# A message-passing layer with a running maximum: four exact lanes of 100,000 edges, a short last pair, one transfer for each load, x loaded earlier at the end, and the norm's small operands in PSUM

## The reference

```python
h = jnp.maximum(_layernorm(x, axis=-1), 0.0)
e_feat = jnp.concatenate([h[src], h[dst], edge_attr], axis=-1)   # 96 features
hid = jax.nn.relu(e_feat @ W1 + b1)                               # 64
v = hid @ W2 + b2                                                 # 32
x_cand = jax.ops.segment_max(v, dst, num_segments=12500)
out = x + jnp.maximum(x_cand, h)
```

## Time and profile before

| what | value |
|---|---|
| median of 3 runs | 3252.11 us (3249.76 to 3254.17) |
| the profiled execution: its own time | 3252.11 us |
| the profiled execution: span from first to last instruction | 3250.3 us |
| PE busy | 3011.4 us, 93% of the span |
| POOL busy | 2432.8 us, 75% |
| DVE busy, ACT busy | 2193.5 us and 2108.6 us, 67% and 65% |
| mean granted TensorE clock | 0.967 of full speed |

### The profile page before, as it was taken

How to read it: one execution, slowest core, us unless ns; L and a number is a source line. 1 busy time by engine, 2 the same in 40 slices (tenths; PEclk the granted TensorE clock), 3 DMA queues, 4 the chain that set the end, 5 groups by cost and what they waited for, 6 DMA issues and landing times.

```text
span 3250.3 us, 56988 instructions
## 1 busy us (share of the span) xinstructions
PE 3011.4 (93%) x19600; PEld 2222.8 (68%) x19600; DVE 2193.5 (67%) x2408; ACT 2108.6 (65%) x2462; POOL 2432.8 (75%) x2558
## 2 busy tenths in 40 slices
PE   6999999999999999999999999999998998999800
PEld 4777677777777777777777777777676776777500
DVE  6221677777777777777777777777676767777623
ACT  2335677777777777777777777776775776777500
POOL 7777777777777777777777777777777777777746
PEclk9999999999999999999999999999999999999955
DMA  9940333333333333333333333333333333333211
GB/s 303 362 128 27 85 100 99 101 102 99 100 98 99 95 99 100 97 98 97 99 101 100 101 97 99 98 97 84 103 99 80 97 76 109 99 98 97 68 47 26
DMA packets 199047, 338.71 MB, mean 104 GB/s; under 512 B 78486, under 2 KB 122520, under 8 KB 198391
## 3 DMA queue, kind: packets, MB, share of 16 engines
q1 hardware_dynamic: 114866, 293.24, 27.3%
q0 software_dynamic: 81568, 41.91, 10.2%
q10 hardware_dynamic: 2464, 2.14, 0.2%
HBM read 228.49 MB, written 108.59 MB: 104 GB/s over the span
## 4 chain that ended last, share of the span: by engine, by line
PE 87%; DMA 4%; issue 3%; POOL 2%; DVE 2%; SPq 1%; ACT 0%; DVEq 0%; POOLq 0%; ACTq 0%
PE ps_rows L689 66%; PE ps_layers L668 4%; PE ps_layers L670 4%; PE ps_layers L704 3%; PE ps_layers L718 3%; PE ps_layers L727 3%; PE ps_layers L708 3%; PE ps_layers L713 2%; POOL gathered_max L560 2%; DMA picks<-picks_dram 2%; DMA gathered_max<-run_max,gather_ix 1%; POOL src_in L491 1%; DVE onehot L927 1%; DMA src_in<-h_dram,src_ix 0%; DMA dst_i<-in_dst_dram 0%
## 5 line engine op out<-in xcount | busy, mean ns | idle before, releaser
L491 POOL DMA_INDIRECT src_in<-h_dram,src_ix x2304 | 2176.7, 945 | 702.1 <-issue 638.4
L689 PE MATMUL ps_rows<-onehot,table 128*128 128x512 f32 x9800 | 2289.5, 393 | 21.7 <-DVE onehot L927 21.6
L689 PEld LDWEIGHTS ps_rows<-onehot,table 128*128 128x128 f32 x9800 | 1831.0, 188 | 495.9 <-issue 107.2
L620 ACT ACTIVATE onehot<-distance 128x1024 fp32r<-128x1024 bf16 x882 | 878.3, 1049 | 700.6 <-PE ps_rows L689 700.6
L615 ACT ACTIVATE distance<-picks,below_column 128x1024 bf16<-128x1024 int16 x882 | 954.8, 1136 | 52.2 <-DMA picks<-picks_dram 52.2
L927 DVE SCALAR_TENSOR_TENSOR onehot<-picks,column,ps_layers 128x1024 fp32r<-128x1024 int16 x392 | 493.1, 1279 | 365.2 <-PE ps_rows L689 339.0
L668 PE MATMUL ps_layers<-ea_t,rows_in 125*128 125x320 bf16 x980 | 269.1, 302 | 26.4 <-DVE rows_in L793 26.4
L969 DVE STREAM_TRANSPOSE ps_layers<-rows_in 128x512 f32<-128x512 f32 x196 | 129.4, 706 | 231.8 <-ACT hid L606 193.9
L670 PE MATMUL ps_layers<-dst_t,rows_in 125*128 125x320 bf16 x980 | 269.0, 301 | 0.0
L606 ACT ACTIVATE hid<-ps_layers,b_col 128x512 f32<-128x512 f32 x392 | 234.5, 675 | 40.2 <-PE ps_layers L718 40.2
L984 DVE TENSOR_TENSOR_SCAN max_t<-mask_in,max_t,ps_layers 128x512 f32<-128x512 bf16 x196 | 250.5, 1278 | 10.7 <-PE ps_layers L727 7.1
(11 more groups left out here) (108 smaller groups left out, 1107.1 us busy)
## 6 DMA issues: line engine op xcount, KB each, us to landing
picks<-picks_dram SPq DMA_DIRECT2D x98, 512.0 KB
run_max<-rows_in SPq DMA_DIRECT2D x98, 512.0 KB
first_rows<-hid SPq DMA_DIRECT2D x100, 500.0 KB
rows_in<-in_edge_attr_dram SPq DMA_DIRECT2D x98, 384.0 KB
rows_in<-first_rows SPq DMA_DIRECT2D x98, 384.0 KB
src_in<-h_dram,src_ix POOLq DMA_INDIRECT x2304
mask_in<-mask_dram SPq DMA_DIRECT2D x98, 192.0 KB
rows_in<-in_edge_attr_dram SPq DMA_DIRECT2D x98, 128.0 KB
```

The costliest lines, as they stand in the source:

```text
L491: pool.indirect_dma_start(out=src_in[:, slot, g, r, :], out_offset=None, in_=rows[:, :], in_offset=bass.IndirectOffsetOnAxis(ap=src_ix[:, ...
L620: nc.scalar.activation(onehot[:, RING_AT[c] + BY_DVE[c] + k, :, :].rearrange("p g w -> p (g w)"), distance[:, k, :], ACT.Relu, bias=1.0, s ...
L689: mm = nc.tensor.matmul(ps_rows[g][side][:, 0:WIDE], table[:, i * SIDES + side, part, :], onehot[:, RING_AT[c] + t, g, :], start=(i + part ...
```

## The change

The lanes become exact quarters of 100,000 edges that start at multiples of LANE. The last pair of each lane then has 672 edges in place of 1024: block g = 0 is full, block g = 1 has 160 edges, of which 32 are gathered (one gather) and 128 looked up. Everything that reads or writes the last pair has a form of its own. With equally spaced lanes a load is one transfer of 128 partitions. At the end x is loaded ahead of the stores of pairs 96 and 97. In the norm the mean and 1 / std are written to PSUM, and ACT takes the squares. SP's loop runs one turn of 14 pairs fewer and the pairs are written out instead. The addition for overlapping lanes in `place_last` goes away.

```diff
-STARTS = [a * ((E - LEN) // (A - 1)) for a in range(A - 1)] + [E - LEN]
...
-LOADS = 2
+LANE = E // A
+STARTS = [a * LANE for a in range(A)]
...
+LAST = LANE - (PAIRS - 1) * 2 * BLK
+LAST_PARTS = LAST // (2 * R)
...
+LAST_GATHERED = LAST - BLK - PICKED
...
+        ps_mean, ps_rstd = (ps_rows[0][n][:, 0:NJ] for n in range(2))
...
-        def row_view(t, a0, a1):
-            return bass.AP(t.tensor, STARTS[a0] * F, [[STEP * F, a1 - a0], [2 * R * F, LANES], [2 * BLK * F, PAIRS], [1, 2 * R * F]])
+        def row_view(t):
+            return bass.AP(t.tensor, 0, [[LANE * F, A], [2 * R * F, LANES], [2 * BLK * F, PAIRS - 1], [1, 2 * R * F]])
...
+        def last_rows(t, start):
+            return bass.AP(t.tensor, (start + LANE - LAST) * F, [[2 * R * F, LAST_PARTS], [1, 2 * R * F]])
...
-            def load_edges(j, slot):
-                for v, lanes in enumerate(lanes_of):
-                    sp.dma_start(ea_rows[chunks(*lanes), slot:slot + 1], ea_view[v][:, :, bass.ds(j, 1)]).then_inc(ea_loaded[slot], D)
+            def load_edges(j, slot, last=False):
+                if last:
+                    for a in range(A):
+                        sp.dma_start(ea_rows[chunk_of_last(a), slot], last_rows(edge_attr, STARTS[a])).then_inc(ea_loaded[slot], D)
+                else:
+                    sp.dma_start(ea_rows[:, slot:slot + 1], ea_view[:, :, bass.ds(j, 1)]).then_inc(ea_loaded[slot], D)
...
-            def store(j, slot):
+            def store(j, slot, last=False):
                 sp.wait_ge(max_turned, j * 2 + 2)
                 sp.sem_inc(loads_begun, 1)
-                sp.dma_start(max_view[:, :, bass.ds(j, 1)], max_rows[:, slot:slot + 1]).then_inc(max_stored[slot], D)
+                if last:
+                    for a in range(A):
+                        sp.dma_start(last_rows(run_max, STARTS[a]), max_rows[chunk_of_last(a), slot]).then_inc(max_stored[slot], D)
+                else:
+                    sp.dma_start(max_view[:, :, bass.ds(j, 1)], max_rows[:, slot:slot + 1]).then_inc(max_stored[slot], D)
...
+            def load_x():
+                sp.wait_ge(tiles_used, PAIRS * TILES)
+                sp.dma_start(x_again[0:PIECE], x_rows[0:PIECE]).then_inc(x_loaded, D)
...
+                if end:
+                    load_x()
+                store(j, slot, last)
...
-            def gather_pair(half, slot, tiles_before):
-                for b in range(BURSTS):
+            def gather_pair(half, slot, tiles_before, last=False):
+                for b in range(BURSTS // 2 + 1 if last else BURSTS):
                     pool.wait_ge(tiles_used, tiles_before + b)
                     pool.sem_inc(gathers_begun, 1)
-                    gather_burst(half, slot, b)
+                    if last and b == BURSTS // 2:
+                        gather_row(half, slot, 1, 0)
+                    else:
+                        gather_burst(half, slot, b)
...
+                if j == SQUARE_AT:
+                    act.wait_ge(table_padded, 1)
+                    act.wait_ge(ln_step, 3)
+                    nc.scalar.activation(squared, centred, ACT.Square).then_inc(ln_step, 1)
...
-                        nc.tensor.matmul(ps_hid[a][g * HID:(g + 1) * HID, cols], w_src[chunk(a), :], src_t[chunk(a), g, :],
+                        nc.tensor.matmul(ps_hid[a][g * HID:(g + 1) * HID, 0:gathered[g]], w_src[chunk(a), :], src_t[chunk(a), g, 0:gathered[g]],
...
-            V.tensor_scalar(mean[:, :], mean[:, :], 1.0 / F, None, ALU.mult).then_inc(ln_step, 1)
+            V.tensor_scalar(ps_mean, mean[:, :], 1.0 / F, None, ALU.mult).then_inc(ln_step, 1)
...
-            V.tensor_tensor(squared, centred, centred, ALU.mult).then_inc(ln_step, 1)
...
-                    V.transpose(by_rows(src_t[:, g, :], GATHERS), src_in[:, k % AHEAD, g, :, :]).then_inc(src_turned, 1)
+                    if last and g == 1:
+                        dve.wait_ge(src_gathered[k % AHEAD][g], turn * (2 * D * GATHERS) + (k // AHEAD) * (D * GATHERS) + D)
+                        V.transpose(src_t[:, g, 0:LAST_GATHERED], src_in[:, k % AHEAD, g, 0, :]).then_inc(src_turned, 1)
```

More of the change, by code:

```diff
@@ L29 @@
 TURNS = PAIRS // AHEAD
-LEN = 2 * PAIRS * BLK
-assert LANES == F == 32 and A * LEN >= E and PAIRS % (2 * AHEAD) == 0
-STARTS = [a * ((E - LEN) // (A - 1)) for a in range(A - 1)] + [E - LEN]
[L33 to L37, removed]
-LOADS = 2
+LANE = E // A
+assert LANES == F == 32 and E == A * LANE and PAIRS % (2 * AHEAD) == 0 and PAIRS // (2 * AHEAD) > 2
+STARTS = [a * LANE for a in range(A)]
+LAST = LANE - (PAIRS - 1) * 2 * BLK
+LAST_PARTS = LAST // (2 * R)
 PICKS = 4
@@ L44 @@
 PICKED = PICKS * LANES
+LAST_GATHERED = LAST - BLK - PICKED
+assert LAST_PARTS * 2 * R == LAST and LAST_GATHERED == LANES
 WIDE = A * PICKED
@@ L167, in build @@
         table_f = work[:, UNITS * P:2 * UNITS * P].rearrange("p (t f) -> p t f", f=P)
-        mean, var, std, rstd = (sb(n, [P, NJ]) for n in ("mean", "var", "std", "rstd"))
+        mean, var, std = (sb(n, [P, NJ]) for n in ("mean", "var", "std"))
         node_i = sb("node_i", [P, NJ], I32)
@@ L360, in load_first @@
[L360 to L366, removed]
+                    sp.dma_start(src_ix[chunk(a), half, :, :, :].rearrange("l s g r -> l (s g) r")[:, 0:blocks],
+                                 ix_view[a][:, bass.ds(j * 2, blocks)]).then_inc(loaded, D)
@@ L452, in feed @@
                     sp.sem_inc(loads_begun, 1)
-                    load_mask(j + 2, slot)
-                store(j, slot)
+                    load_mask(j + 2, slot, before_last)
+                if end:
+                    load_x()
+                store(j, slot, last)
             DOUBLE_TURNS = PAIRS // (2 * AHEAD)
-            with sp.Fori(0, DOUBLE_TURNS - 1) as i:
+            with sp.Fori(0, DOUBLE_TURNS - 2) as i:
                 for k in range(2 * AHEAD):
                     feed(i * (2 * AHEAD) + k, k, i)
[L460 to L468, removed]
+            for turn in range(DOUBLE_TURNS - 2, DOUBLE_TURNS):
+                for k in range(2 * AHEAD):
+                    j = turn * 2 * AHEAD + k
+                    feed(j, k, turn, loads=j + 2 < PAIRS, picks=j + 3 < PAIRS, indices=j + 2 * AHEAD - IX_AT < PAIRS, end=j == PAIRS - 2,
+                         before_last=j == PAIRS - 3, last=j == PAIRS - 1, last_indices=j + 3 * AHEAD - IX_AT == PAIRS)
             all_stored(sp)
             for a in range(1, A):
-                sp.dma_start(carry[:, a - 1, :], bass.AP(run_max.tensor, ((a - 1) * LEN + STEPS[a - 1]) * F, [[0, P], [1, F]])).then_inc(carry_loaded, D)
+                sp.dma_start(carry[:, a - 1, :], bass.AP(run_max.tensor, (STARTS[a] - 1) * F, [[0, P], [1, F]])).then_inc(carry_loaded, D)
             for hb in range(1, NHB, 2):
@@ L519, in gather_turn @@
                     pool.sem_inc(gathers_begun, 1)
-                    gather_pair(half, slot, turn * (AHEAD * TILES) + (slot + 2 - AHEAD) * TILES)
+                    gather_pair(half, slot, turn * (AHEAD * TILES) + (slot + 2 - AHEAD) * TILES, last and slot == AHEAD - 1)
             pool.wait_ge(early_ix_loaded, A * D)
@@ L548, in _ @@
                 gather_turn(i * 2 + 2, 0, i + 1)
-            gather_turn(TURNS - 1, 1, TURNS // 2)
+            gather_turn(TURNS - 1, 1, TURNS // 2 + 1, last=True)
             all_stored(pool)
@@ L692, in look_up, with layer_one @@
                     mm.then_inc(tiles_used, 1)
[L695 to L696 removed]
+            def layer_one(j, slot, ahead, last):
                 wait(pe, max_scanned, j * 2)
@@ L729, in layer_two, with pair @@
                 mm.then_inc(v_summed, 1)
-            def pair(j, slot, ahead=True):
-                layer_one(j, slot, ahead)
+            def pair(j, slot, ahead=True, last=False):
+                layer_one(j, slot, ahead, last)
                 if ahead:
@@ L748, in _ @@
             for slot in range(2):
-                pair(PAIRS - 2 + slot, slot, ahead=False)
+                pair(PAIRS - 2 + slot, slot, ahead=False, last=slot == 1)
         @block_.vector
@@ L1009, in place_last @@
                 dve.wait_ge(place_step, n)
-                V.tensor_tensor(gather_at[:, :], gather_at[:, :], tmp[:, :], ALU.add).then_inc(place_step, 1)
+                V.tensor_tensor(gather_at[:, :], last[:, :], tmp[:, :], ALU.add).then_inc(place_step, 1)
                 n += 1
@@ L1040, in _, with pair @@
             turn_edges(0, 0, 0)
-            def pair(j, k, turn, again, ahead=True, following=True):
+            def pair(j, k, turn, again, ahead=True, following=True, last_next=False):
                 slot = k % 2
```

105 lines of the change are left out of this document (57 added, 48 removed).

## The result

The changed kernel takes **3276.18 us** (median of 6 runs, 3274.10 to 3277.16) where the kernel before takes 3251.88 (6 runs, 3249.76 to 3254.17): ratio 1.0074, 95% interval 1.0064 to 1.0085. It is 24.3 us slower; the forecast was 3234.0, 18 us faster, with a range that ended at 3246. The profiled execution spans 3275.3 us, 25.0 more than before. The difference is 0.7%, small but clear of the scatter of the runs, which do not overlap.

The account below looks back on a forecast made before the run. The kernel looks PE-bound, but its time is set by when POOL ends. Span 3250.3 - 3.0 (pair 95) - 10.1 (pair 97) - 5.0 (last store) = 3232.2, so 3234.0 us; forecast range 3229 to 3238, with rivals 3225 to 3246.

Parts of the forecast that it names:

- `place_last` shorter, the two extra loads on ACT's queue: Small instructions in front of waits for PE, priced at 0.
- E: Slower by the loop's four-lane load shape: picks 8 us late, 3 us in each of some 95 pairs; 3470; chance 0.08.
- POOL's start, what is kept at pair 7: Three gathers beside long DVE instructions stop losing 7.2 us; POOL leaves pair 7's wait about 2.1 early, bounds 0 to 7.2.
- norm's move, at the end: Norm inputs in PSUM unblock POOL's early gathers; the 2.1 us kept makes pair 95's last gather go earlier.
- pair 95: Its last gather goes 2.1 us earlier and may land up to 2.6 sooner; 3.0 us taken.
- pair 97, to the last store: 11 fewer gathers end DVE's wait, PE's third layer-one group starts 9.5 us earlier, fewer columns save 0.6: together 10.1 us.
- last store to carry: Four transfers of 21 partitions in place of 128 shorten the last store's 10.4 us by 5.0, bounds 1.1 to 5.5.
- tile wait: POOL's second burst of pair 7 waits for tile 27, done at 363.5, and stands there some 5 us.
- Squares on ACT: One count of the search starts up to some 2 us late, at most 1 felt; taken as 0.
- Rival A: All of POOL's 7.2 us from the start comes out at the end: 3229; chance 0.08.
- B: The last store gains little, 1.1 us or below in place of 5.0: 3238 to 3240; chance 0.13.
- C: Earlier loads of x delay POOL's last gathers, DVE waits 2 to 8 us again: 3236 to 3242; chance 0.09.

Follow-up runs that it names:

- e2b: Kernel before with each pick_i load covering 97 partitions in place of 98, plus three small loads for the last: 3299.83 us, ratio 1.0129 to the kernel before.
- e1b: Changed kernel with each pick_i load split into 96 and 1 partitions, e1 repeated on another chip: 3237.98 us, ratio 0.9942 to the kernel before.
- e5b: e1 with the norm as in the kernel before (mean and 1 / std in SBUF, squares on DVE): 3232.88 us, ratio 0.9946 to the kernel before.
- e9: e1 with eleven more gathers in the last pair, into places nothing reads, ahead of the real last one: 3245.32 us, ratio 0.9980 to the kernel before.
- e8: e1 with the four loads of x behind the last store, as before: time unusable because of the chip; store to carry 3.79 us.
- e6: e1 with POOL's gathers waiting for the tiles of one pair less: 3227.81 us, ratio 0.9926 to the kernel before.
- e7: e6 with the norm as in the kernel before: 3231.43 us, ratio 0.9941 to the kernel before.
- experiment 3: Changed kernel with pick_i loaded in 94 and 3 partitions, or one lane in 97 and the others in 96 and 1: all six runs on unusable chips.
- e10: e1 with the last of four pick_i lanes loaded in one transfer of 97 partitions: time unusable because of the chip; ACT's table load at 43.06 us.
- e10b: e10 once more: time unusable because of the chip; ACT's table load at 42.96 us.
- e1: Changed kernel with each pick_i load split into 96 and 1 partitions, on a chip unusable for time; ACT's table load at 31.35 us.

## Why the prediction was wrong

**The step that failed** is "`place_last` shorter, the two extra loads on ACT's queue. Small instructions in front of waits for PE: 0." That sentence prices the two small loads that are added, and says nothing of the four big ones in front of them, which went from 98 partitions to 97 for the sake of a last pair of another shape: a term put at nothing without a reason. What the runs showed in its place: the four issues hold ACT's queue for 49.6 us in place of 4.1, ACT's count of the search, on which PE's search and with it the whole loop waits, begins 43 us late (table load at 75.28 in place of 32.03), and 42 to 45 us are lost to the end (e2b with the shape alone loses 42.8; e1b without it is 43 faster than the changed kernel, by the ratios to the kernel before). Of all rivals none had it. E, the one for slower, looked at the shape of the loop's loads and at a wait in every pair, and there nothing was lost: from the start of pair 0 to that of pair 96 PE takes 2712.8 us before and in e1b. The prediction applied the rule on engines to 96 and 21 partitions, and not to 97.

Point by point for the rest, e1b against the kernel before, by one trace each, taken on two chips:

| term | predicted | measured | from |
|---|---|---|---|
| gathers beside the norm last 0.94 | yes | yes | timeline above |
| POOL's start, what is kept at pair 7 | 2.1 | -0.3 | 366.21 against 365.89 |
| norm's move, at the end | part of 3.0 | 0 | e5b |
| pair 95 | 3.0 | 0, in e5b 3.0 | PE starts pair 96 at 3070.92 and 3067.86, before at 3070.85 |
| pair 97, to the last store | 10.1 | 11.5 | 3107.85 to 3096.37; e9 |
| last store to carry | 5.0 | 6.7 | 10.44 to 3.75; e8 |
| sum | 18.1 | 18.2 | the spans are 18.1 apart |

So what the prediction worked out for the rest of the change was about right in size (by medians 19.1 us, with 14 to 24 in the interval, and 18.2 in e5b), but that it agrees to 0.1 is luck: 3.0 too much, 1.4 and 1.7 too little, and pair 95 alone differs by 3 us between traces, with the landing of its last gather. Of the 11.5 for pair 97, 9.7 are the earlier start of the third group (3096.19 to 3086.53). The remaining 1.8 goes with the clock, which the prediction left out: behind its gap the kernel before runs the last groups at a granted clock of 0.50, the lower level, and they take 1.59, 1.98 and 1.96 us; in e1b it is 0.98, and they take 0.89, 1.09 and 1.09. The 0.6 that was expected from fewer columns in the first of them doesn't show: with the short block e9 takes 1.56 at nearly the same clock.

The tile wait was seen as the thing that eats POOL's 7.2 us, which was right (e6 and e7), and mis-sized by 2: POOL's burst comes 2.9 us after the start of pair 2's look-ups and not 2.1, and in e1b PE reaches these 1.7 us later than before (363.29 against 361.59), because the groups before them run at a granted clock of 0.68 where it was 1.00. Nothing in the change explains that drop, and in the kernel after it is 1.00 at this place. Squares on ACT cost nothing that the end shows. Rival A needed the wait gone; without it 3.6 to 4.4 of 7 came. B and C did not happen: the store gained more than forecast, and x, at 3071 in e1b, made no wait for pair 97.

## What to carry to other kernels

When an edit changes the extent of a transfer, look at the divisors of the new outermost count before its bytes: 98 to 97 partitions turned four issues of together 4.1 us into 49.6 us (experiment 3 has the rule), and 96 + 1 repaired it. Such a load costs whoever stands behind it in the issuing queue, not itself, so read that queue to the first instruction that another engine waits for. And a gain on the bounding engine counts only past its last tie to another one: 7 us won before a wait were worth 0, and 3.6 with the wait loosened (e6, the fastest version here, 23 us under the kernel before).

## What the runs showed of the hardware

- Four loads of 97 partitions by 1 KB and two small ones, 784 packets of 512 bytes, take 63.8 us on ACT's queue, 81 ns a packet in the mean, 500 ns from 12 to 22 us (DMA share 1.01) and 25 ns from 62 to 66 us (share 0.18); the same bytes on 98 partitions take 20 us.
- A queue blocks behind such a load even when only one is in it: 23.2 to 24.0 us for the next two small issues (e10, e10b).
- Beside a long DVE instruction with two SBUF inputs one indirect gather lasts 3.0 to 3.7 us in the norm, and 0.94 when one input is in PSUM. The change leaves others: in e1b a gather still lasts 4.17 us beside the comparison that makes the mask (L880, both inputs in SBUF).
- The last store in four transfers of 21 partitions lands in 3.75 us, in one of 128 it took 10.44.
- The last gather of one pair landed 4.2 to 10.0 us after its issue in six traces, at the same place of the program.
- The same program takes 3251 to 3257 us on some chips and 4347 to 4452 on others. There the granted clock is 0.87 for 0.97. From 1000 to 2000 us PE's second group of layer one (L746) takes 1035 ns a matmul in e1, with 72.1 us of idle time in front that is put down to its own issue, and 614 ns with none in e1b. What causes it is open.
